# A mixture-of-experts scatter-add into one DRAM sum instead of two, one scatter in flight at a time

## What is computed

```python
scores = softmax(x @ gate.T)                  # 4096 x 64
topk_w, topk_i = top 6 of 64 experts, out of the best 3 of 8 groups
slot = expert * 96 + min(position in the expert's list, 95)
buf[slot] = x[token]                          # 64 experts x 96 rows x 256; the last one written wins slot 95
out = (silu(buf @ Wg.T) * (buf @ Wu.T)) @ Wd.T
y = sum over the 6 choices of out[slot] * topk_w
x = x + y + shared_expert(x)
```

## Time and profile before

| what | us |
|---|---|
| median of the runs (837.95 to 842.42) | 840.81 |
| the profiled execution, its own time | 842.78 |
| its span, first to last instruction | 841.0 |
| TensorE busy | 676.1 |
| VectorE busy | 482.0 |
| GpSimd busy | 378.1 |
| ScalarE busy | 338.5 |
| 64 scatters, GpSimd time for making their DMAs | 118.2 |
| 64 gathers, the same | 62.3 |

### The profile page before, as it was taken

The page is one execution under the profiler, slowest core; times in us unless marked ns, Lnnn a source line. Parts: engine busy times, 40 slices in busy tenths (PEclk is TensorE's granted clock), DMA queues, the critical chain, the costliest instruction groups (busy, mean ns, idle before and its releaser), DMA issues. The chain is left out here.

```text
span 841.0 us, 16829 instructions
## 1 busy us (share of the span) xinstructions
PE 676.1 (80%) x6353; PEld 482.3 (57%) x6353; DVE 482.0 (57%) x1086; ACT 338.5 (40%) x636; POOL 378.1 (45%) x354
## 2 busy tenths in 40 slices
PE   2699999998988788888745999799999987773083
PEld 1266666676766566665412556477887765553062
DVE  3267776677868777778445999533333332321057
ACT  2477777766767646755121332112222211110000
POOL 5122222125343423431121832847776777776454
PEclk9899999998999989999756999899999999997555
DMA  7234444665532223210018000138999988953298
GB/s 218 27 59 79 79 79 77 99 98 100 100 73 62 47 45 76 48 44 29 5 44 257 2 0 1 42 96 224 239 235 228 231 211 212 225 127 40 24 302 303
DMA packets 125376, 94.30 MB, mean 112 GB/s; under 512 B 73137, under 2 KB 109169, under 8 KB 125297
## 3 DMA queue, kind: packets, MB, share of 16 engines
q1 hardware_dynamic: 96368, 74.57, 35.1%
q0 software_dynamic: 23552, 14.21, 10.2%
q10 hardware_dynamic: 5376, 4.46, 1.7%
HBM read 60.26 MB, written 24.44 MB: 101 GB/s over the span
## 5 line engine op out<-in xcount | busy, mean ns | idle before, releaser
L1229 POOL DMA_INDIRECT sum_d<-nz,tokens x64 | 118.2, 1847 | 46.8 <-issue 14.6
L724 DVE TENSOR_REDUCE mx<-Sc 128x16 f32<-128x1024 f32 x64 | 77.9, 1217 | 37.8 <-PE Sc L401 37.5
L1056 PE MATMUL bank<-xnT,sgu_sb 128*128 128x512 f32 (+1 forms) x192 | 86.9, 601 | 11.8 <-PEq L1588 11.8
L1111 PE MATMUL bank<-xT,wgu_sb 128*88 128x96 f32 x1024 | 95.1, 246 | 0.3 <-ACT xT L1180 0.3
L1279 DVE TENSOR_TENSOR hid<-sil,bank 88x192 f32<-88x192 f32 x64 | 22.4, 350 | 118.2 <-ACT sil L1186 88.6
L1111 PEld LDWEIGHTS bank<-xT,wgu_sb 128*88 128x88 f32 x1024 | 89.4, 157 | 0.6 <-issue 0.5
L600 ACT COPY ET<-ring 128x512 f32<-128x512 f32 x128 | 69.5, 589 | 44.0 <-PE ring L413 41.8
L429 PEld LDWEIGHTS O<-vbd,ET 128*64 128x64 f32 x2048 | 69.2, 142 | 25.9 <-issue 17.3
L413 PE MATMUL ring<-ident,E 128*128 128x128 f32 x512 | 73.8, 290 | 12.5 <-ACT E L639 11.5
L728 DVE TENSOR_TENSOR E<-Sc,mx 128x1024 f32<-128x1024 f32 x64 | 78.4, 1225 | 6.9 <-DVE mx L724 0.5
L401 PE MATMUL Sc<-kbd,qT 64*64 64x256 f32 x1024 | 76.4, 404 | 6.7 <-DMA kbd<-kT 6.7
(11 more groups left out here) (149 smaller groups left out, 1144.1 us busy)
## 6 DMA issues: line engine op xcount, KB each, us to landing
wgu_sb<-in_wgu_dram SPq DMA_DIRECT2D x64, 352.0 KB
wd_sb<-in_wd_dram SPq DMA_DIRECT2D x64, 176.0 KB
sum_d<-zeros SPq DMA_DIRECT2D x16, 524.0 KB, 6.4
y<-sum_d SPq DMA_DIRECT2D x16, 512.0 KB, 8.8
kbd<-kT SPq DMA_DIRECT2D x248, 32.0 KB, 2.1
X<-in_x_dram SPq DMA_DIRECT2D x8, 512.0 KB, 6.4
rows_d<-xhT SPq DMA_DIRECT2D x8, 512.0 KB, 3.0
out_dram<-X ACTq DMA_DIRECT2D x8, 512.0 KB, 5.2
```

Source lines behind the costliest of these rows:

```text
L724: nc.vector.reduce_max(mx[:, m % 2, :], sc, AX.X).then_inc(s_mx, 1)
L1056: last = nc.tensor.matmul(out[0:m, :], sgu[:, e, k * MS + m0:k * MS + m0 + m], xnT[:, e, TOK * g:TOK * (g + 1)], start=e == 0, stop=e == 1)
L1111: last = nc.tensor.matmul(GP[e % 2][0:MH, CAP * u:CAP * (u + 1)], wgu[:, j, 4 * MH * c + MH * u:4 * MH * c + MH * (u + 1)], xT[:, e % 2, c ...
L1229: pool.indirect_dma_start(w["sums"][e % 2], bass.IndirectOffsetOnAxis(ap=tokens[0:CAP - 1, e:e + 1], axis=0), outs[0:CAP - 1, e % EB, :], ...
```

## The change

The two sums become one. Scatter e waits for scatter e - 1, and it writes all 96 rows of its buffer: a new list `targets` is `tokens` with the entry of slot 95 replaced by the last dump row, so that row 95's sum is never read. The final phase loads one sum, and VectorE adds it to x without the addition on POOL. Only half the zeros are written in the attention phase. `lastrow` is a column of zeros with 4191 in its last place; `own` is one but for its last place, where it is zero.

```diff
             def zero_rows(q):
-                for y in w["sums"]:
-                    sp.dma_start(y.rearrange("r e -> (r e)").rearrange("(q p a b) -> q p a b", q=NG, p=128, b=NZ)[q],
-                                 zeros[:, 0:NZ].unsqueeze(1).to_broadcast([128, ZROW // NZ, NZ])).then_inc(s_zd, 16)
+                sp.dma_start(w["sum"].rearrange("r e -> (r e)").rearrange("(q p a b) -> q p a b", q=NG, p=128, b=NZ)[q],
+                             zeros[:, 0:NZ].unsqueeze(1).to_broadcast([128, ZROW // NZ, NZ])).then_inc(s_zd, 16)
...
             def scatter(e):
                 pool.wait_ge(s_o, e + 1)
-                if e >= 2:
-                    pool.wait_ge(s_s[e % 2], 16 * (e // 2))
-                pool.indirect_dma_start(w["sums"][e % 2],
-                                        bass.IndirectOffsetOnAxis(ap=tokens[0:CAP - 1, e:e + 1], axis=0),
-                                        outs[0:CAP - 1, e % EB, :], None, compute_op=ALU.add).then_inc(s_s[e % 2], 16)
+                if e >= 1:
+                    pool.wait_ge(s_s, 16 * e)
+                pool.indirect_dma_start(w["sum"],
+                                        bass.IndirectOffsetOnAxis(ap=targets[:, e:e + 1], axis=0),
+                                        outs[:, e % EB, :], None, compute_op=ALU.add).then_inc(s_s, 16)
...
             add(GE - 1)
+            pool.wait_ge(s_list, 2)
             for e in range(NE):
...
-            for k in range(2):
-                pool.wait_ge(s_s[k], 16 * NE // 2)
+            pool.wait_ge(s_s, 16 * NE)
...
                 if e >= EB:
-                    dve.wait_ge(s_s[e % 2], 16 * ((e - EB) // 2 + 1))
+                    dve.wait_ge(s_s, 16 * (e - EB + 1))
...
             nc.vector.tensor_copy(tokens[:], P[0][0:CAP, 0:NE]).then_inc(s_list, 1)
+            nc.vector.tensor_scalar(targets[:], P[0][0:CAP, 0:NE], own[:], lastrow[:], ALU.mult,
+                                    ALU.add).then_inc(s_list, 1)
...
             for g in range(NG):
-                sp.dma_start(y0[:, GT * g:GT * (g + 1), :], sums[0][g]).then_inc(s_y[g], 16)
-                sp.dma_start(y1[:, GT * g:GT * (g + 1), :], sums[1][g]).then_inc(s_y[g], 16)
+                sp.dma_start(y[:, GT * g:GT * (g + 1), :], total[g]).then_inc(s_y[g], 16)
...
-        @block.gpsimd
-        def _(pool):
-            for g in range(NG):
-                rows = slice(GT * g, GT * (g + 1))
-                pool.wait_ge(s_y[g], 32)
-                nc.gpsimd.tensor_tensor(y0[:, rows, :], y0[:, rows, :], y1[:, rows, :], ALU.add).then_inc(s_sum, 1)
-
...
-                dve.wait_ge(s_sum, g + 1)
+                dve.wait_ge(s_y[g], 16)
                 dve.wait_ge(s_xo, 2 * g + 2)
                 rows = slice(GT * g, GT * (g + 1))
-                nc.vector.tensor_tensor(X[:, rows, :], X[:, rows, :], y0[:, rows, :], ALU.add).then_inc(s_x, 1)
+                nc.vector.tensor_tensor(X[:, rows, :], X[:, rows, :], y[:, rows, :], ALU.add).then_inc(s_x, 1)
...
                 nc.gpsimd.memset(mem["own"][:], 1.0).then_inc(s_half, 1)
                 nc.gpsimd.memset(mem["lastone"][:], 0.0).then_inc(s_half, 1)
-                pool.wait_ge(s_half, 2)
-                for m, op, fill in ((mem["own"], ALU.not_equal, 0.0), (mem["lastone"], ALU.not_equal, 1.0)):
+                nc.gpsimd.memset(mem["lastrow"][:], 0.0).then_inc(s_half, 1)
+                pool.wait_ge(s_half, 3)
+                for m, op, fill in ((mem["own"], ALU.not_equal, 0.0), (mem["lastone"], ALU.not_equal, 1.0),
+                                    (mem["lastrow"], ALU.not_equal, float(NT * 128 + CAP - 1))):
                     nc.gpsimd.affine_select(out=m[:], in_=m[:], compare_op=op, fill=fill, base=-(CAP - 1),
                                             pattern=[[0, 1]], channel_multiplier=1).then_inc(s_half, 1)
```

More of the change, by code:

```diff
@@ L333, in _ @@
                 sp.wait_ge(s_wst[k], 16 * NG // 2)
-            sp.wait_ge(s_zd, (2 * NG + 1) * 16)
+            sp.wait_ge(s_zd, (NG + 1) * 16)
         @block.tensor
@@ L969, in sem @@
         return ctx.enter_context(nc.semaphore(f"m_{name}"))
-    X, ident, xnT, key, wt, kw, nz, top2, both, thr, top, tokf, slot, mark, lastk, sg, su, hT, sh, tokens = (
+    X, ident, xnT, key, wt, kw, nz, top2, both, thr, top, tokf, slot, mark, lastk, sg, su, hT, sh, tokens, targets = (
         mem[k] for k in ("X", "ident", "xnT", "keys", "wt", "kw", "nz", "top2", "both", "thr", "top", "tokf", "slot",
-                         "mark", "lastk", "sg", "su", "hT", "sh", "tokens"))
-    xg, xT, sil, hid, wcol, own, lastone = (mem[k] for k in ("xg", "xT", "sil", "hid", "wcol", "own", "lastone"))
+                         "mark", "lastk", "sg", "su", "hT", "sh", "tokens", "targets"))
+    xg, xT, sil, hid, wcol, own, lastone, lastrow = (
+        mem[k] for k in ("xg", "xT", "sil", "hid", "wcol", "own", "lastone", "lastrow"))
     outs = nz[0:CAP, :].rearrange("p (j e) -> p j e", e=E)
@@ L1019, in moe_phase @@
     s_o = sem("weighted")
-    s_s = [sem(f"added{k}") for k in range(2)]
+    s_s = sem("scattered")
     s_l = [sem(f"last_stored{j}") for j in range(EB)]
@@ L1362, in sem @@
         return ctx.enter_context(nc.semaphore(f"f_{name}"))
-    X, wt, lastsb, y0, y1 = (mem[k] for k in ("X", "wt", "lastsb", "y0", "y1"))
+    X, wt, lastsb, y = (mem[k] for k in ("X", "wt", "lastsb", "y"))
     P = mem["banks"]
@@ L1369, in final_phase @@
     s_xo = sem("over_added")
-    s_sum = sem("sum")
     s_x = sem("result")
     s_out = sem("stored")
-    sums = [y[0:NT * 128, :].rearrange("(g t p) e -> g p t e", p=128, t=GT) for y in w["sums"]]
+    total = w["sum"][0:NT * 128, :].rearrange("(g t p) e -> g p t e", p=128, t=GT)
     out = w["out"].rearrange("(g t p) e -> g p t e", p=128, t=GT)
@@ L1441, in decoder_layer @@
         rows_d = nc.dram_tensor("rows_d", (NT * 128 + CAP, E + NE), F32, kind="Internal").ap()
-        sums_d = [nc.dram_tensor(f"sum{k}_d", (NT * 128 + CAP, E), F32, kind="Internal").ap() for k in range(2)]
+        sum_d = nc.dram_tensor("sum_d", (NT * 128 + CAP, E), F32, kind="Internal").ap()
         lasts_d = nc.dram_tensor("lasts_d", (NE, E), F32, kind="Internal").ap()
@@ L1451, in decoder_layer @@
         w = dict(gate=gate, x=x, ctx=ctx_rows, wq=wq, bq=bq, wk=wk, bk=bk, wv=wv, bv=bv, wc=wc, bc=bc, rows=rows_d,
-                 sums=sums_d, lasts=lasts_d, wgu=wgu, wd=wd, out=out)
+                 sum=sum_d, lasts=lasts_d, wgu=wgu, wd=wd, out=out)
         mem["keys"] = sb("keys", [128, NT * 64])
@@ L1559, in decoder_layer @@
         mem["tokens"] = sb("tokens", [CAP, NE], I32)
+        mem["targets"] = sb("targets", [CAP, NE], I32)
         w["sgu_sb"] = sb("sgu_sb", [128, 2, 2 * MS])
@@ L1585, in decoder_layer @@
                             ("xT", [128, 2, 2, CAP]), ("sil", [MH, 2, 2 * CAP]), ("hid", [MH, 2, 2, CAP]),
-                            ("wcol", [CAP, EB]), ("own", [CAP, 1]), ("lastone", [CAP, 1])):
+                            ("wcol", [CAP, EB]), ("own", [CAP, 1]), ("lastone", [CAP, 1]), ("lastrow", [CAP, 1])):
             mem[name] = sb(name, shape)
@@ L1603, in decoder_layer @@
         mem["lastsb"] = sb("lastsb", [128, E])
-        mem["y0"] = sb("y0", [128, NT, E])
-        mem["y1"] = sb("y1", [128, NT, E])
+        mem["y"] = sb("y", [128, NT, E])
         final_phase(nc, ctx, mem, w)
```

## The result

The changed kernel takes 900.05 us (median of 4 runs, 898.34 to 902.51) where the kernel before takes 839.45 (4 runs on the same chips): 1.072 of it, 95% interval 1.067 to 1.077, 60.6 us slower. The forecast was 883 us with a range of 852 to 935.

A forecast was written before the change was run, and what follows sets the result against it. TensorE bound the expert phase up to 660 us, POOL's loop at or just under its limit; 49.4 - 2.3 - 4.1 - 1 + 0.2 = +42.2 on the median 840.8 gave 883 us, range 852 to 935.

The forecast's parts named there:

- One in flight, a turn is descriptors plus turnaround: POOL's expert loop: each scatter waits for the last, turns of 4.55 us while weights load, 3.8 after; +49.4 us.
- 5 engines for 95 rows, 16 for 96: Scatter's DMA: 95 rows go 19 each over 5 engines, 96 rows 6 each over 16; packets fall from 320 to 112.
- Rival C: Scatter's DMA: the spread over 5 engines does not change; +194 us on the intervals, about 1030 us; chance 0.05.
- The turnaround: From a scatter's descriptor end to the waiting scatter's start: 5.0 to 3.5 us under weight loads, 4.24 to 2.75 after.
- Rival B: Expert loop: landing as quick under load as on the quiet chip, 3.54 us per turn, 828 us; chance 0.08.
- Descriptors: POOL's descriptor writing per scatter falls from 1.85 to 1.05 us, near the gather's 0.94, as empty packets go.
- Rival A: POOL's descriptor writing stays at 1.85 us because accumulating, not empty packets, makes it dear; 934 us; chance 0.16.
- The last scatter 2.3 us shorter: End of the expert phase: the last scatter saves 0.8 us of descriptors and 1.5 of transfer, -2.3 us.
- The end, -4.1: Final phase: POOL's additions and half the loads go, VectorE's last additions take 1.21 us each; -4.1 us.
- Zero fills, -1: Attention phase: eight of 16 zero fills on SyncE go, ahead of key blocks; -1 us (0 to -3).
- the small terms: Fewer zero fills, -1 us, and one more memset and constant on POOL before the phase's barrier, +0.2 us.
- rival D: Expert phase: TensorE, busy 64%, drops to its lower clock; some 60 turns at 5.9 us, about 960 us; chance 0.05.

The follow-up runs named there:

- experiment 1: The kernel before with scatters of 96 rows from the list targets, still two sums and two scatters in flight: 806.63 us, 0.959 of the kernel before.
- experiment 6: Two sums and 96 rows as in experiment 1, but scatter e waits for scatter e - 1, one in flight: 907.44 us.
- Experiment 2: The changed kernel with scatters of 95 rows instead of 96: 1010.2 us.
- experiment 3: The changed kernel with scatters that write instead of adding, the sum over the choices left out: 858.85 us.
- experiment 4: The changed kernel with scatters of rows 0 to 47 only, contributions of slots 48 to 94 left out: 887.2 us.
- experiment 5: The kernel before with the final phase loading only the first sum, added on VectorE, odd experts' part left out: 836.34 us, 0.9943 of the kernel before.
- experiment 7: The kernel of experiment 1 with a GpSimd drain between the last scatter's issue and the wait for its landing: 805.18 us, 0.958 of the kernel before.

## Why the prediction was right, step by step

- **One in flight, a turn is descriptors plus turnaround: right.** Experiments 1 and 6 differ in this wait alone, and 101 us hang on it.
- **5 engines for 95 rows, 16 for 96: right.** There are 112 packets per scatter and 10240 in all, as forecast. Experiment 2 shows what it is worth. This is also why the changed kernel isn't at 1010 us, and the Trainium skill's rule on the number of engines (DMA: Bandwidth & Descriptors, "Why a DMA increments its semaphore by 16 and not by 1") fits the packet counts on both sides of the change. Rival C falls.
- **The turnaround: right in size.** Forecast 3.5 while weights load and 2.75 after; the first 50 intervals are (794.07 - 558.1) / 50 = 4.72 us, which is 1.44 and 3.28, the last 13 are (848.63 - 794.07) / 13 = 4.20, 1.44 and 2.76, and 2.65 to 2.7 at the very end. What fell is the transfer alone. By the packet records the last scatter's last packet ends 3.12 us after its descriptors in the kernel before, 1.57 in the changed one, 1.10 in experiment 3 and 1.38 in experiment 4; against the quiet turnarounds of 4.24, 2.67, 2.22 and 2.44 this leaves 1.1 us each time. Rival B had the quiet chip's 2.6 us throughout, with 0.94 of descriptors: its 2.6 is nearly met at the very end, but while weights load the turnaround is 3.28. The 2.2 us cited for it from the Trainium skill (DMA: Bandwidth & Descriptors, "Anatomy of one DMA — SWDGE (gpsimd) path"), an estimate, falls short of 2.67 even on the quiet chip; 2.21 is what scatters that only write come to (experiment 3).
- **Descriptors: the term that was mis-sized.** 1.05 was taken, near the gather; it is 1.44, inside the bounds 0.94 and 1.87. The step that failed is "the 209 empty packets explain the difference". They explain 0.41 of 0.91 us; the other 0.5 is adding (experiments 3, 4). Over 63 turns that is 0.39 x 63 = 24.6 us too little, against 0.22 x 50 = 11 too much for the turnaround: 276.9 forecast, 290.5 measured. That these two errors partly cancel is luck. Rival A, with all of it due to adding, was half right.
- **The last scatter 2.3 us shorter: wrong.** Its landing is shorter, but the phase's end eats that up: the first load comes 10.56 us after the last scatter's start instead of 9.59. So this term is +1.0, not -2.3; that GpSimd takes longer to close the phase (last section) was no term of the sum.
- **The end, -4.1: right.** It is -4.7 in the trace. Two pairs share everything that bears on the end but the final phase's code: the kernel before and experiment 5, 13.1 against 9.1 us, and experiment 6 and the changed kernel, 12.1 against 8.3. They give 4.0 and 3.8. Where the 1 us between 13.1 and 12.1 comes from stays open.
- **Zero fills, -1:** not to be seen. With 8 of them the first scatter starts at 556.7 to 559.5 (the changed kernel and experiments 2, 3, 4), with 16 at 557.9 to 558.8 in experiments 1, 5, 6, 7.
- **The sum:** the intervals are 13.6 us above their term and the last scatter 3.3; the end is 0.6 below, the small terms 0.8 above (0 for -1 and +0.2), and TensorE's part of the final phase adds 0.1. That is 42.2 + 17.2 = 59.4.
- **TensorE's clock (rival D):** the expected 1.00 was wrong, it fell to 0.95 and 0.89 in the two stages. It cost nothing that the turns show: the 8th scatter's buffer was weighed 14 us before its scatter, those from the 17th on at least 28 us before. A turn's length is given by POOL's two numbers, and rival D falls.
- **What the kernel before was bound by:** the prediction had TensorE as first up to 660 us, and waits for transfers as rare, 9.7 us in 6. Both readings were wrong. Two rows of before, in order of time:

```profile
595.60 0.48 DVE L1289 TENSOR_SCALAR nz<-bank,wcol 96x256 f32<-96x256 f32 x1
602.92 1.85 POOL L1229 DMA_INDIRECT sum_d<-nz,tokens  x1 [1.22 <-DVE wcol L1272]
```

The first weighs the 12th expert's result, the second is its scatter, 6.8 us after the buffer was ready, and yet idle for 1.22 us: only scatter e - 2 can have held it, whatever the label says. For the 21st scatter the lead is 14.6 us, from the 30th on 19 to 22. Counted so, 35 of the 63 scatters after the first waited for scatter e - 2, 26 us in all above the 0.3 between two issues. Experiment 1 changes nothing but the scatters, and up to 660 us 33 of them start where 26 did before. So POOL's loop and its scatters set the pace there as well, while TensorE ran ahead on rows gathered earlier. This didn't enter the sum.

## What to carry to other kernels

A wait for the last transfer instead of the one before it makes the loop's turn as long as the full way of one transfer. Read that way out of the trace (from the end of the descriptors to the start of what had to wait), multiply it by the turns, and set it against what the second buffer costs at the end: here 101 us against 4 to 5. Check a wait's label against what the code waits for, and against when that was done. Count the packets of an indirect DMA: here, small ones beyond one per engine went with rows on 5 engines instead of 16, and one padding row may be worth more than the change around it. Take a change apart before it is judged: one half of this one makes the kernel 4% faster, the other makes it 12% slower than that.

## What was not expected of the hardware

- An adding indirect scatter of 96 rows costs 1.44 us of GpSimd's descriptor writing, a plain one 0.93; 48 rows instead of 96 take off only 0.07, and the 208 packets more of 95 rows add 2 ns each.
- Between the last scatter's descriptors and the next phase's first load, across the barrier, lie 7.7 to 7.8 us with 95-row scatters (before, experiments 2 and 5), 9.2 to 9.3 with 96 rows (the changed kernel, 1 and 6), and 12.4 and 12.7 in experiments 3 and 4, although the landing is earlier in each. GpSimd's DRAIN at the phase's end, an instruction of its sequencer in the trace, starts once the last scatter has landed and ends 0.25 us before the first load: it lasts 3.8 us in the first group, 6.8 in the second and 10.5 in both of the third, where POOL's queue had 23552, 10240 and 6144 or 7168 packets in all. A drain put right behind the last issue ran beside the landing and left 0.05 us for the one at the barrier (experiment 7). Why the drain is longer after fewer packets was not found out.
- A stage that shows TensorE 100% busy was sped up without touching TensorE's work: up to 660 us the scatters start 3.81 us apart in the kernel before and 3.18 in experiment 1.
